# A Perceiver layer on one core: the drain reordered with the last chunk ahead of the first ranks, and the second expert layer's bias through PE with eight tile buffers

## The reference

```python
x = x + xattn(layernorm(x), ctx, Wq, Wk, Wv, Wo, bo)     # 16 heads, 257 context rows a sequence
x = x + time_mix(layernorm(x), mix_k, mix_v, mix_r, W_key, W_value, W_receptance, W_output, decay, first)
x = x + ffn(layernorm(x), Wr, br, W1, b1, W2, b2)

def ffn(x, Wr, br, W1, b1, W2, b2):                      # 8 experts, 128 -> 512 -> 128
    logits = x @ Wr.T + br
    e = argmax(logits, axis=-1)                          # one expert for each token
    h = relu(x @ W1[e].T + b1[e])
    return h @ W2[e].T + b2[e]
```

## Time and profile before

| | us |
|---|---|
| median of three runs | 949.33 (947.11 to 950.98) |
| the profiled execution, own time | 950.45 |
| its span, first to last instruction | 948.7 |
| PE busy | 858.7 (91%) |
| DVE busy | 806.1 (85%) |
| POOL busy | 788.3 (83%) |
| ACT busy | 683.1 (72%) |

### The profile page before, as it was taken

How to read it: one execution, slowest core, us unless ns; L and a number is a source line. 1 busy time by engine, 2 the same in 40 slices (tenths; PEclk the granted TensorE clock), 3 DMA queues, 4 the chain that set the end, 5 groups by cost and what they waited for, 6 DMA issues and landing times.

```text
span 948.7 us, 28634 instructions
## 1 busy us (share of the span) xinstructions
PE 858.7 (91%) x8486; PEld 712.5 (75%) x8486; DVE 806.1 (85%) x2058; ACT 683.1 (72%) x1956; POOL 788.3 (83%) x1218
## 2 busy tenths in 40 slices
PE   7999999999999999999999999999999874429992
PEld 7777787887888888888888888888887663427882
DVE  5899879898989898989898989989898967657882
ACT  3877787777878787887877787877887662308881
POOL 5798898989898989998999989898989754654885
PEclk9999999999999999999999999999999985659997
DMA  9122222222211221222221222112120032111220
GB/s 251 26 60 73 61 61 61 61 61 61 60 59 59 59 59 59 75 62 75 64 78 59 59 59 59 59 59 59 59 60 28 1 122 105 43 51 49 73 64 13
DMA packets 56704, 60.90 MB, mean 64 GB/s; under 512 B 8750, under 2 KB 50609, under 8 KB 56640
## 3 DMA queue, kind: packets, MB, share of 16 engines
q1 hardware_dynamic: 54144, 55.84, 20.2%
q0 software_dynamic: 2496, 4.26, 1.4%
HBM read 37.65 MB, written 23.34 MB: 64 GB/s over the span
## 4 chain that ended last, share of the span: by engine, by line
PE 35%; POOL 32%; issue 14%; DVE 11%; ACT 4%; POOLq 1%; SPq 1%; DMA 0%; DVEq 0%; ACTq 0%
POOL Pn L1040 12%; PE bank L392 7%; PE bank L443 5%; PE bank L414 4%; PE bank L436 4%; POOL cT L1031 3%; PE bank L404 3%; PE bank L420 3%; POOL out_dram L1430 3%; POOL chi L1021 2%; POOL e12p L1047 2%; DVE Tl L885 2%; POOL clo L1025 2%; POOL e12p L1050 1%; POOL yb L1424 1%
## 5 line engine op out<-in xcount | busy, mean ns | idle before, releaser
L813 ACT ACTIVATE Pe<-bank,nmax 128x257 f32<-128x257 f32 x512 | 241.5, 472 | 108.2 <-DVE nmax L881 89.2
L1040 POOL TENSOR_TENSOR Pn<-Pe,rsum 128x1028 f32<-128x1028 f32 x128 | 243.1, 1900 | 36.3 <-DVE rsum L905 28.8
L392 PE MATMUL bank<-cT,qh 96*128 96x257 f16 x1024 | 184.3, 274 | 5.7 <-ACT Pe L813 4.1
L885 DVE TENSOR_TENSOR Tl<-bank,Th 128x1024 f16<-128x1024 f32 x128 | 155.4, 1214 | 2.3 <-ACT Th L802 1.9
L443 PE MATMUL bank<-identf,Pn 128*128 128x128 f32 x1024 | 152.7, 275 | 0.6 <-POOL Pn L1040 0.4
L802 ACT ACTIVATE Th<-bank 128x512 f16<-128x512 f32 x256 | 141.0, 593 | 9.1 <-PE bank L443 9.0
L392 PE MATMUL bank<-cT,ql 96*128 96x257 f16 x512 | 139.1, 272 | 0.0
L392 PEld LDWEIGHTS bank<-cT,qh 96*128 96x128 f16 x1024 | 97.6, 97 | 44.9 <-issue 9.6
L443 PEld LDWEIGHTS bank<-identf,Pn 128*128 128x128 f32 x1024 | 114.2, 141 | 9.1 <-POOL Pn L1040 2.1
L881 DVE TENSOR_REDUCE nmax<-bank 128x2 f32<-128x514 f32 x128 | 88.1, 688 | 21.0 <-PE bank L392 19.9
L894 DVE TENSOR_REDUCE nmax<-bank 128x1 f32<-128x257 f32 x256 | 105.0, 412 | 0.0
(11 more groups left out here) (229 smaller groups left out, 2431.3 us busy)
## 6 DMA issues: line engine op xcount, KB each, us to landing
sorted_rows<-fill SPq DMA_DIRECT2D x30, 589.5 KB, 3.8
rawT<-in_dram SPq DMA_DIRECT2D x32, 385.5 KB, 4.5
raw<-in_dram SPq DMA_DIRECT2D x32, 384.0 KB, 5.1
xs<-sorted_rows SPq DMA_DIRECT2D x23, 131.0 KB, 2.2
R<-in_dram SPq DMA_DIRECT2D x4, 512.0 KB, 5.8
Z<-last_rows SPq DMA_DIRECT2D x128, 2.2 KB
w1r<-in_dram SPq DMA_DIRECT2D x4, 512.0 KB, 8.0
w2fr<-in_dram SPq DMA_DIRECT2D x4, 512.0 KB, 9.2
```

The lines of the kernel that those rows point to most:

```text
L392: last = nc.tensor.matmul(bank[SB[t]][:, 0:M], w[:, par, b, t * P:(t + 1) * P], cT[:, s4, c, 0:M], start=(k == 0), stop=(k == 2))
L813: nc.scalar.activation(Pe[:, n_par(j + 1), t, :], bank[SB[t]][:, 0:M], ACT.Exp, bias=nmax[:, n_par(j + 1), t:t + 1], accum_out=sums[:, n_p ...
L885: nc.vector.tensor_tensor(Tl[:, n_par(j - 1), :, :], psum[:, 4:4 + MC, :], Th[:, n_par(j - 1), :, :], ALU.subtract).then_inc(s_Tl, 1)
L1040: nc.gpsimd.tensor_tensor(Pn[:, par, :, :], Pe[:, par, :, :], rsum[:, par, :].unsqueeze(2).broadcast_to([P, QT, M]), ALU.mult)\
```

## The change

- **Bias.** `b2b` and the POOL add are gone. SP loads `b2` into two partitions (`b2r`) early. In `pool_route_tables`, in step n = 5 of the pipeline, POOL makes `b2p` in five instructions: zeros in 128 partitions, in partition 0 the high fp16 part of `b2`, in partition 1 the low part. In the tile stage PE starts each second layer with two matmuls of 128 columns, all ones (`onesh`) times `b2p` of the expert, into the same banks. DVE adds the residual from `xs` directly and casts the row numbers from `xs`.
- **Buffers.** `xs` has eight buffers (`XN`); it is freed by `out`, not by `xn` and `yb`. POOL stores tile s-2 in step s, not s-3, and loads no experts.
- **Drain.** PE: the last chunk's transposes go between logits(2) and T(4), its keys between T(5) and logits(4), its sum between logits(5) and the first ranks. ACT: the copies and `ek` move accordingly, and the norms of units 4 and 5 move to DVE (`dve_norm`). DVE: `mix_dx` and `mix_xm` of the last chunk go ahead of the logits of unit 3. The first four `dve_w` move from LIT+1 to behind `pk`.

The diff, with its shorter parts (allocations, waits that follow from these) left out:

```diff
@@ -77,6 +77,7 @@
...
     UN = 4
+    XN = 2 * UN
     PK = 8
@@ -305,6 +308,10 @@
...
         nmr = asb("nmr", [P, G])
+        b2r = asb("b2r", [2, E, C])
+        b2h = asb("b2h", [2, E, C], F16)
+        b2l = asb("b2l", [2, E, C])
+        b2p = asb("b2p", [P, E, C], F16)
         arena.close()
@@ -345,14 +351,13 @@
...
 
-        xs = lsb("xs", [P, UN, SUB, RW])
+        xs = lsb("xs", [P, XN, SUB, RW])
         xsn = lsb("xsn", [P, 2, SUB, C])
...
         hl = lsb("hl", [P, UN, FC, TR], F16)
-        yb = lsb("yb", [P, UN, SUB, C + 1])
         yout = lsb("yout", [P, UN, SUB, C])
@@ -646,6 +651,15 @@
...
                                     pattern=[[1, P]], channel_multiplier=-1).then_inc(s_ftab, 1)
+            wait(nc.gpsimd, s_b2, 16)
+            nc.gpsimd.memset(b2p[:, :, :], 0.0).then_inc(s_b2p, 1)
+            nc.gpsimd.tensor_copy(b2h[:, :, :], b2r[:, :, :]).then_inc(s_b2p, 1)
+            wait(nc.gpsimd, s_b2p, 2)
+            nc.gpsimd.tensor_tensor(b2l[:, :, :], b2r[:, :, :], b2h[:, :, :], ALU.subtract).then_inc(s_b2p, 1)
+            wait(nc.gpsimd, s_b2p, 3)
+            nc.gpsimd.tensor_copy(b2p[0:2, :, :], b2l[:, :, :]).then_inc(s_b2p, 1)
+            wait(nc.gpsimd, s_b2p, 4)
+            nc.gpsimd.tensor_copy(b2p[0:1, :, :], b2h[0:1, :, :]).then_inc(s_b2p, 1)
             nc.gpsimd.iota(R[:, :, C], pattern=[[P, G]], base=0, channel_multiplier=1,
@@ -1230,6 +1245,7 @@
...
             wait(nc.vector, s_f["xT"], i - 1)
+            wait(nc.vector, s_f["xn"], i)
             for t in range(CT):
@@ -1331,6 +1347,7 @@
...
             sp.dma_start(brb[:, :], br.rearrange("(o e) -> o e", o=1).broadcast_to([P, E])).then_inc(s_rw, 16)
+            sp.dma_start(b2r[:, :, :], b2.rearrange("(o e) d -> o e d", o=1).broadcast_to([2, E, C])).then_inc(s_b2, 16)
             sorted_fill = sorted_rows.rearrange("(f p k) c -> p f (k c)", p=P, k=FR)
@@ -1342,7 +1359,6 @@
...
             sp.dma_start(b1T[:, :], b1T_d).then_inc(s_small, 16)
-            sp.dma_start(b2b[:, :, 0:C], b2.rearrange("(o e) d -> o e d", o=1).broadcast_to([P, E, C])).then_inc(s_w3, 16)
 
@@ -1354,9 +1370,9 @@
...
             for s in range(NT):
-                u = s % UN
-                wait(sp, s_t["xn"], s - UN + 1)
-                wait(sp, s_t["yb"], s - UN + 1)
+                u = s % XN
+                wait(sp, s_t["xn"], s - XN + 1)
+                wait(sp, s_t["out"], s - XN + 1)
                 sp.dma_start(xs[:, u, :, :], sorted_blocks[bass.ds(block_of[s], 1), :, :, :].rearrange("o p m c -> p (o m) c"))\
@@ -1414,24 +1429,15 @@
...
                 s = UN * it + u
-                if exists(s - 3, NT):
-                    wait(pool, s_t["out"], s - 2)
-                if exists(s + 1, NT):
-                    w = (u + 1) % UN
-                    e = expert(u + 1)
-                    wait(pool, s_xs[w], 16 * (it + 1 + (u + 1) // UN))
-                    pool.wait_ge(s_w3, 16)
-                    nc.gpsimd.tensor_tensor(yb[:, w, :, :], xs[:, w, :, 0:C + 1],
-                                            b2b[:, bass.ds(e, 1), :].broadcast_to([P, SUB, C + 1]), ALU.add)\
-                        .then_inc(s_t["yb"], 1)
-                if exists(s - 3, NT):
-                    v = (u - 3) % UN
+                if exists(s - 2, NT):
+                    v = (u - 2) % UN
+                    wait(pool, s_t["out"], s - 1)
                     for m in range(SUB):
...
 
-            over_tiles(pool, pool_tile)
+            over_tiles(pool, pool_tile, routed=False)
 
@@ -1447,11 +1453,14 @@
...
             drain(act_step, LIT, 5, 7)
-            for i in range(3, UA):
-                act_unit_norm(i)
-                act_unit_x3T(i - 1)
-            act_unit_x3T(UA - 1)
-            drain(act_step, LIT + 1, -1, 5)
+            act_unit_norm(3)
+            act_unit_x3T(2)
+            drain(act_step, LIT + 1, -1, 1)
+            act_unit_x3T(3)
+            act_unit_x3T(4)
+            drain(act_step, LIT + 1, 1, 2)
+            act_unit_x3T(5)
+            drain(act_step, LIT + 1, 2, 5)
             act_std(GA, GA + CT, 1)
@@ -1521,13 +1530,21 @@
...
             drain(pe_step, LIT, 5, 6)
-            for i in range(2, UA):
-                pe_unit_T(i)
-                pe_unit_logits(i - 1)
-            pe_unit_logits(UA - 1)
+            pe_unit_T(2)
+            pe_unit_logits(1)
+            pe_unit_T(3)
+            pe_unit_logits(2)
+            drain(pe_step, LIT, 6, 7)
+            drain(pe_step, LIT + 1, -1, 1)
+            pe_unit_T(4)
+            pe_unit_logits(3)
+            pe_unit_T(5)
+            drain(pe_step, LIT + 1, 1, 2)
+            pe_unit_logits(4)
+            pe_unit_logits(5)
+            drain(pe_step, LIT + 1, 2, 3)
             pe_rank(0, GA, 0)
-            drain(pe_step, LIT, 6, 7)
-            drain(pe_step, LIT + 1, -1, 6)
+            drain(pe_step, LIT + 1, 3, 6)
             pe_unit_T(UA)
@@ -1571,12 +1588,16 @@
...
                     pe.wait_ge(s_w3l, 2 * E)
+                    wait(pe, s_b2p, 5)
+                    for m in range(SUB):
+                        nc.tensor.matmul(bank[6 + m][:, 0:C], onesh[:, :],
+                                         b2p[:, bass.ds(e, 1), :].rearrange("p o c -> p (o c)"), start=True, stop=False)
                     for f in range(FC):
...
                                                         w[:, bass.ds(e, 1), f * P:(f + 1) * P].rearrange("p o c -> p (o c)"),
-                                                        start=(f == 0 and k == 0), stop=(f == FC - 1 and k == 2))
+                                                        start=False, stop=(f == FC - 1 and k == 2))
                     last.then_inc(s_t["y"], 1)
@@ -1606,15 +1627,20 @@
...
             drain(dve_step, LIT, 6, 7)
-            for i in range(UA):
+            dve_unit_logits(0)
+            dve_norm(4)
+            dve_unit_logits(1)
+            dve_norm(5)
+            dve_unit_logits(2)
+            mix_dx(nc.vector, LIT + 1, 0)
+            mix_xm(nc.vector, LIT + 1, 1)
+            for i in range(3, UA):
                 dve_unit_logits(i)
...
             dve_hot(0, GA)
-            dve.wait_ge(s_ftab, 12)
+            dve.wait_ge(s_ftab, 11)
             dve_rank(0, GA, 0)
             drain(dve_step, LIT + 1, -1, 1)
-            mix_dx(nc.vector, LIT + 1, 0)
-            mix_xm(nc.vector, LIT + 1, 1)
             drain(dve_step, LIT + 1, 1, 2)
@@ -1626,7 +1652,6 @@
...
             mix_states(nc.vector, LIT + 1, 5)
-            dve_w(range(0, 4))
             drain(dve_step, LIT + 1, 6, 7)
@@ -1663,7 +1688,7 @@
...
             nc.vector.tensor_copy(pk[:, :], pkf[:, :]).then_inc(s_te, 1)
-            dve_w(range(4, 2 * E))
+            dve_w(range(0, 2 * E))
             dve.wait_ge(s_te, 1)
@@ -1675,16 +1700,16 @@
...
                 if exists(s - 2, NT):
-                    w = (u - 2) % UN
-                    wait(dve, s_t["yb"], s - 1)
+                    w, x = (u - 2) % UN, (s - 2) % XN
+                    wait(dve, s_xs[x], 16 * ((s - 2) // XN + 1))
                     wait(dve, s_store[w], 16 * SUB * (it + (u - 2) // UN))
-                    nc.vector.tensor_copy(idx[:, w, :], yb[:, w, :, C])
+                    nc.vector.tensor_copy(idx[:, w, :], xs[:, x, :, C])
                     wait(dve, s_t["y"], s - 1)
-                    nc.vector.tensor_tensor(yout[:, w, :, :], psum[:, 6:6 + SUB, 0:C], yb[:, w, :, 0:C], ALU.add)\
+                    nc.vector.tensor_tensor(yout[:, w, :, :], psum[:, 6:6 + SUB, 0:C], xs[:, x, :, 0:C], ALU.add)\
                         .then_inc(s_t["out"], 1)
                 if exists(s + 3, NT):
-                    v, w = (u + 1) % 2, (u + 3) % UN
-                    wait(dve, s_xs[w], 16 * (it + 1 + (u + 3) // UN))
+                    v, w = (u + 1) % 2, (s + 3) % XN
+                    wait(dve, s_xs[w], 16 * ((s + 3) // XN + 1))
                     wait(dve, s_t["xT"], s + 2)
```

More of the change, by code:

```diff
@@ L247, in perceiver_layer_kernel @@
         s_f = {n: sem("f_" + n) for n in ("xn", "xT", "xc", "lg", "rt")}
-        s_xs = [sem(f"s_xs{u}") for u in range(4)]
+        s_xs = [sem(f"s_xs{u}") for u in range(XN)]
+        s_b2 = sem("s_b2")
+        s_b2p = sem("s_b2p")
         s_store = [sem(f"s_store{u}") for u in range(4)]
-        s_t = {n: sem("t_" + n) for n in ("xn", "xT", "xh", "xl", "h", "hr", "hh", "hl", "y", "yb", "out")}
+        s_t = {n: sem("t_" + n) for n in ("xn", "xT", "xh", "xl", "h", "hr", "hh", "hl", "y", "out")}
         block = top.enter_context(nc.Block())
@@ L322, in perceiver_layer_kernel @@
         b1T = lsb("b1T", [P, E * FC])
-        b2b = lsb("b2b", [P, E, C + 1])
         kk = lsb("kk", [P, E, TOK // TR])
@@ L694, in act_unit_norm @@
             wait(nc.scalar, s_f["xT"], i - 1)
+            wait(nc.scalar, s_f["xn"], i)
             wait(nc.scalar, s_nmr, 1 + max(0, i - UA + 1))
@@ L1396, in _ @@
             pool.wait_ge(s_res, GB * G)
```

(1 more changed line is left out.)

## The result

The changed kernel took 952.36 us (median of 19 runs, 949.12 to 955.19), the kernel before 949.41 (19 runs, 947.11 to 951.80): a ratio of 1.0027, 95% interval 1.0019 to 1.0036, or 1.8 to 3.4 us slower. 952.36 lies inside the forecast's range (943 to 956.5).

What follows compares the result with a forecast made beforehand. POOL was taken to bound the tiles and to have no slack in the pipeline, where PE and POOL balance. Tables +6.3, drain +0.5, tiles -1.4 and tail -4.2 gave +1.2, so 950.5 us, range 943 to 956.5.

Steps and rivals of the forecast that it cites:

- What bounds it: Tile stage bound by POOL, never idle; in the pipeline PE and POOL balanced, with no slack at the second `Pn`.
- Tables, +6.3: Early pipeline: five POOL instructions, 6.1 us, make PE wait for `Pn` twice; 6.3 us lost (4.0 to 9.0).
- The 0.4 added to the 5.9: Early pipeline: 0.4 us added to PE's 5.9 us delay from the tables, giving +6.3.
- The rival of cheap copies on one or two partitions: Pipeline: copies 0.5 each, subtraction 1.2, tables 4.0 us, about 3.5 stay; tiles at PE's pace; total 943.8; chance 0.22.
- Drain, +0.5: Reordered drain: logits and first ranks 2.5 us later, DVE rid of 1.95, `ekv` 0.5 later (-3.5 to +2.5).
- The rival in which the clock rises before the logits of unit 6: Drain: denser work brings PE to 2.4 GHz, warm-up and logits halve, -3.5 us; total 946.5; chance 0.10.
- The step that freeing DVE of four `dve_w` brings nothing: Drain: 2.4 us of DVE freed, yet PE's warm-up matmuls hold the path, so nothing gained.
- Tiles, -1.4: Tile stage: a step takes 3.20 us instead of 3.28, over 18 steps -1.4 us (-3.2 to +2).
- the 3.10: Tile step without store collisions: 3.05 us without POOL, plus half of 0.11 for the bias products on PE.
- The rival of `idx` behind the second store: Tiles, DVE: second store holds `idx` up to 0.97; mean step 3.5, +4.0 instead of -1.4; total 956; chance 0.18.
- Tail, -4.2: After the last `xsn` transposes: POOL without backlog ends its stores at +16.3 us instead of 20.5 (-5.3 to -3.0).
- The sum: Whole kernel: +6.3 + 0.5 - 1.4 - 4.2 = +1.2 us, 951.6 for a like execution, 950.5 for the median.

Runs made afterwards that it cites:

- dummy_tab: The kernel before plus the load of `b2r` and the five table instructions in pipeline step 5, result unused; 958.98 us, ratio 1.0082.
- drain_only: The kernel before with only the new order of the drain; ratio 1.0001.
- no_warm: The changed kernel with tables behind the scatters, minus the eight warm-up matmuls ahead of the last chunk's output product; 943.76 us, ratio 0.9906 to the kernel before.
- no_warm2: As no_warm, with the six warm-up matmuls behind the output product taken out as well; 942.33 us, ratio 0.9910 to the kernel before.
- no_stores: The changed kernel with tables behind the scatters, POOL storing only the last four tiles; 946.12 us, one run.

## Why the prediction was right, and where it wasn't

*What bounds it.* Right for the pipeline: POOL has no slack there, which dummy_tab shows by itself, where 6.3 us of added work arrive at PE as 5.97. In the tiles POOL ran 3.3 to 3.7 behind `yout` and now runs 0.8 to 1.1 behind it, but as a bound it stood little above the next one: taking its add away brought about 0.13 a step, of which the bias products on PE took back 0.075, and taking its stores away as well brought another 0.04.

*Tables, +6.3.* Right in size and mechanism: 6.30 on POOL where 6.1 was summed; the memset 0.95 (0.9), the subtraction 2.12 (2.0), the copies 1.03 (0.95). The 0.4 added to the 5.9 is a term that no run shows. What the changed kernel shows is a granted clock of 0.50 from 75 to 78 us, behind the first wait, where PE had to wait for `Pn` again anyway, and of 1.00 from 83 to 88, behind the second; the last transposes of `Pn` are 5.46 late, not 6.3. The rival of cheap copies on one or two partitions did not come: they took 1.03 on two and on one, not 0.5, and the subtraction on two took 2.12 where `Pn`, as wide and on 128, takes 1.89.

*Drain, +0.5.* Its mean over the profiles is +0.4, made up as forecast: logits later by 2.1 (forecast 2.5; 31.95 against 29.81 in the means), and from there to `ekv` 10.30 instead of 12.02 in every profile, 1.7 less (forecast 1.95). But single logits come at 29.4 to 33.7. I treated the clock as one case with one price, where it is a draw in each execution; against that spread the mean of +0.4 is no proof. The rival in which the clock rises before the logits of unit 6 did not come: after has 0.50 from 799 to 817. The step that freeing DVE of four `dve_w` brings nothing, since the warm-up holds the path, is borne out for the new order as a whole: without the warm-up 1.9 us come out.

*Tiles, -1.4.* -1.0 measured, 3.226 for 3.20. The step that failed is what holds the pace above 3.10: 3.20 was 3.10 and 0.1 for stores that meet `hl`. They do meet, in most tiles, but the stage without stores still has 3.19, so the failing term is the 3.10: the 3.05 of two undisturbed steps was no measure of a mean over 18. I had read two short steps of a pattern that has long ones too. The rival of `idx` behind the second store did not happen: `idx` has a median of 0.16 (0.36 before), by a margin of 0.04 in the row above.

*Tail, -4.2.* -3.6. POOL still has a backlog of one tile at the end: its last four stores start 1.28 apart from 937.26 on, the last of them 3.9 after the last `yout`; the last `yout` itself comes 0.1 later after the transposes than before. *From `pk` to the counted steps*, 0.7 came that I had not in the sum; all eleven kernels without the add of `yb` show 27.3 to 27.7 there, the three with it 28.0 to 28.3.

*The sum.* +1.2 forecast, +1.1 in the profiled execution: a hit by luck. Inside the span the terms come to +0.07; the other 1.05 lie outside the span, for which I had put nothing. The medians say +2.95. Of that 0.7 is the mean outside the span (2.48 in the 19 runs after, 1.75 in those of before that list their spans). The other 2.2 lie inside the span, and the pair of profiles hides them: the profiled execution of after was short (span 948.8; mean of the 19: 950.0), that of before long (950.45; median 949.41). In which stretch they arise stays open.

## What to carry to other kernels

Set-up work belongs where its engine waits, and the profile says where: the same five instructions cost 6 us ahead of a saturated step and nothing that shows behind the scatters, which turned a loss of 0.3% into a gain of 0.55%. A warm-up that stands ahead of a product on the path is a cost to be weighed against the work that runs at the full clock after it; here it took 3.55 us and gave 0.65, and it hid what a reordering had earned behind `ekv`. One profile of a stretch whose clock varies is one draw: five to eight of them were needed to see that the reordering ahead of `ekv` earned nothing that shows. The kernel with the tables behind the scatters and no warm-up there (no_warm, 943.76, ratio 0.9906, and no_warm2, 0.9910) beats both kernels.

## What the runs showed of the hardware

- The same instructions took 39.7 to 44.0 us from one profile to the next, with a mean granted clock of 0.88 to 0.71 up to the last logits; in the old order 41.5 (three profiles, within 0.01), 41.8 and 42.9, with 0.81 to 0.82, 0.77 and 0.72.
- POOL's instructions can slow a DVE instruction with one tensor input too: four normalisations took 4.10 us instead of 1.12 beside a memset, a cast and a subtraction.
- An indirect store of POOL that met `hl` on DVE ended 0.84 after it and took 1.65 us; with none beside it a store takes 0.98.
- A CAST on 2 partitions x 1024 took 1.03, a COPY on 1 partition 1.03, a memset on 128 partitions x 1024 0.95.
- The time outside the span is 1.70 to 1.88 in all runs of before, drain_only and dummy_tab, and 2.04 to 3.10 in every kernel without the add of `yb` that has all its stores (1.72 in the one run of no_stores). Up to a microsecond of the change stands in no trace; its cause stays open.
